# Trip of q, k, v and the attention output through memory: whole rows per block in place of strided pieces, with the features in another order

## The reference

```python
def _L1_attn_ref(x, Wqkv, Wproj, bproj):          # N_HEADS = 16, SCALE = 8.0
    qkv = jnp.einsum('bnm,fm->bnf', x, Wqkv)
    qkv = qkv.reshape(b, n, N_HEADS, -1)
    q, k, v = (qkv[..., :dh], qkv[..., dh:2 * dh], qkv[..., 2 * dh:])   # dh = 16
    scores = jnp.einsum('bnhd,bngd->bnhg', q, k) / SCALE
    attn = jax.nn.softmax(scores, axis=-1)
    out = jnp.einsum('bnhg,bngd->bnhd', attn, v)
    return jnp.einsum('bni,mi->bnm', out.reshape(b, n, -1), Wproj) + bproj

x = _layernorm(x + _L0_attn_ref(x, ...))
x = _layernorm(x + _L0_ffn_ref(x, ...))
x = _layernorm(x + _L1_attn_ref(x, ...))
x = _layernorm(x + _L1_ffn_ref(x, ...))
```

## Time and profile before

| | |
|---|---|
| runs | 1348.04, 1350.33, 1350.30 us; median 1350.3 |
| profiled execution | 1349.4 us, span 1347.6 us, granted clock 0.891 of full |
| busy in the span | PE 87%, DVE 70%, ACT 54%, POOL 42% |
| DMA | 90.64 MB in 94009 packets, most of them of 512 bytes |
| loads of 128 KB from `scratch_qkv` | 192 |
| stores of 512 KB to `scratch_qkv` | 48 |

### The profile page before, as it was taken

The page is one execution under the profiler, slowest core; times in us unless marked ns, Lnnn a source line. Parts: engine busy times, 40 slices in busy tenths (PEclk is TensorE's granted clock), DMA queues, the critical chain, the costliest instruction groups (busy, mean ns, idle before and its releaser), DMA issues.

```text
span 1347.6 us, 31178 instructions
## 1 busy us (share of the span) xinstructions
PE 1167.3 (87%) x12264; PEld 748.0 (56%) x12264; DVE 937.1 (70%) x2124; ACT 722.6 (54%) x1145; POOL 571.8 (42%) x882
## 2 busy tenths in 40 slices
PE   6688899998989999998999989898999988897464
PEld 4444466655665546655566556655566555654452
DVE  3544578677775868767775778668686777755866
ACT  3223375347753575547853477545754477544653
POOL 2235435335354355245354355354462352551124
PEclk8689898799979998799988999799987998799557
DMA  5000092203902075201902056021932029026430
GB/s 188 16 1 16 18 166 23 80 9 101 127 2 79 17 167 54 66 15 68 168 2 80 9 115 113 17 64 33 174 31 64 1 87 133 2 64 114 75 96 32
DMA packets 94009, 90.64 MB, mean 67 GB/s; under 512 B 7110, under 2 KB 83144, under 8 KB 93608
## 3 DMA queue, kind: packets, MB, share of 16 engines
q1 hardware_dynamic: 82008, 77.24, 29.3%
q0 software_dynamic: 2064, 6.69, 1.6%
q10 hardware_dynamic: 9792, 4.72, 1.4%
HBM read 46.68 MB, written 41.94 MB: 66 GB/s over the span
## 4 chain that ended last, share of the span: by engine, by line
PE 57%; DVE 18%; DMA 7%; issue 6%; ACT 5%; POOL 4%; ACTq 1%; SPq 1%; DVEq 0%; POOLq 0%
PE bank L1994 54%; DVE keys L1640 2%; DVE stats L1384 2%; DMA bt<-scratch_o 2%; DVE x L1525 2%; DVE gelu L1642 2%; POOL rs L655 2%; DMA scratch_o<-stage 2%; PE bank L2004 1%; ACT x L996 1%; DVE ct L1353 1%; DMA keys<-scratch_qkv 1%; ACTq L966 1%; ACT part L873 1%; DVE x L1708 1%
## 5 line engine op out<-in xcount | busy, mean ns | idle before, releaser
L1994 PE MATMUL bank<-we,at 128*128 128x512 f16 x1536 | 373.7, 403 | 1.9 <-DVE x L1525 1.9
L1994 PEld LDWEIGHTS bank<-we,at 128*128 128x128 f16 x1536 | 154.4, 102 | 194.6 <-issue 41.6
L670 POOL TENSOR_TENSOR part<-part 128x512 f32<-128x512 f32 x64 | 84.2, 1316 | 276.5 <-ACTq L1022 276.5
L873 ACT ACTIVATE part<-bank,wexp 128x256 f32<-128x256 f32 x256 | 104.3, 470 | 159.6 <-PE bank L1994 102.9
L1525 DVE SCALAR_TENSOR_TENSOR x<-bank,wexp,x 128x256 f32<-128x256 f32 x256 | 122.7, 479 | 53.0 <-PE bank L1994 46.5
L1994 PE MATMUL bank<-bt,wqkv 128*128 128x512 f16 x576 | 137.3, 380 | 20.8 <-DVE stage L1353 12.3
L996 ACT ACTIVATE x<-x,nm,rs 128x256 f32<-128x256 f32 x184 | 100.3, 593 | 69.3 <-POOL nm L658 68.1
L1353 DVE TENSOR_TENSOR stage<-bank,stage 128x512 f16<-128x512 f32 x110 | 74.4, 686 | 82.5 <-ACT stage L873 82.2
L651 POOL TENSOR_SCALAR nm<-mv 128x2 f32<-128x2 f32 x128 | 33.4, 261 | 207.1 <-DVE mv L1389 201.5
L1994 PE MATMUL bank<-keys,blockdiag 128*128 128x16 f16 x3072 | 97.5, 193 | 21.8 <-DVE blockdiag L1554 10.0
L1994 PEld LDWEIGHTS bank<-keys,blockdiag 128*128 128x128 f16 x3072 | 96.1, 103 | 26.4 <-issue 14.5
(11 more groups left out here) (212 smaller groups left out, 2275.4 us busy)
## 6 DMA issues: line engine op xcount, KB each, us to landing
scratch_qkv<-stage SPq DMA_DIRECT2D x39, 512.0 KB, 3.3
ct<-scratch_qkv SPq DMA_DIRECT2D x112, 128.0 KB, 6.5
x_in<-in_x_dram SPq DMA_DIRECT2D x32, 256.0 KB, 2.7
bt<-scratch_o SPq DMA_DIRECT2D x16, 512.0 KB, 4.1
keys<-scratch_qkv SPq DMA_DIRECT2D x61, 128.0 KB, 6.0
out_dram<-x POOLq DMA_DIRECT2D x24, 256.0 KB, 2.7
scratch_qkv<-part SPq DMA_DIRECT2D x8, 512.0 KB, 7.8
scratch_o<-stage SPq DMA_DIRECT2D x32, 128.0 KB, 3.5
```

Of the source, the lines that this page charges most:

```text
L670: pool.tensor_tensor(part[:, 0:2, :], part[:, 0:2, :], part[:, 2:4, :], ALU.add)\
L873: return act.activation(dst, src, ACT.Copy, scale=scale)
L1994: ins = pe.matmul(dst, lhs, rhs, start=(n == 0), stop=(n == len(terms) - 1))
```

## The change

The rows of the weights are put in another order on the host, so that within a block of 128 the features go by dimension, then head (q, k), or by head, then half of the dimensions (v). The block is stored as pieces of 512 bytes, 8 a partition, to a place r, p, n; read back as 128 rows of 4096 bytes, row 16 r + d then holds dimension d of group r for 8 heads. Each tensor comes back in two loads of 512 KB. The output makes the opposite way: two stores of whole rows, and two loads in pieces of 512 bytes. All of them are on SP; ACT's and POOL's issues go. The wait on POOL for v keeps its place and now counts two loads.

```diff
+            def half_of(home, ft):
+                return home[:, 2 * C * (ft % 2):2 * C * (ft % 2 + 1)]
...
+        def by_feature(memory):
+            return memory.rearrange("a m -> (a m)").rearrange("(r p n) -> p r n", r=T, p=P)
+        def qkv_block(ft):
+            return scratch_qkv[P * ft:P * (ft + 1)]
...   b_f and b_flast on SP
-                sp.dma_start(scratch_qkv[P * ft:P * (ft + 1)], slots[s]).then_inc(stored[s], 16)
+                sp.dma_start(by_feature(qkv_block(ft)), slots[s].rearrange("p (r n) -> p r n", r=T)).then_inc(stored[s], 16)
...
+            def load_block(b, ft, home, loaded):
+                sp.wait_ge(*f_stored(b, ft))
+                sp.sem_inc(waits_held, 1)
+                sp.dma_start(half_of(home, ft), qkv_block(ft)).then_inc(loaded, 16)
             def b_loadq(b):
+                if 0 < b < NB - 1:
+                    sp.wait_ge(ff_full, 4 * b)
                 for ft in (0, 1):
-                    (8 loads, or 4 for the last batch, on q_src[:, :, r, :])
+                    load_block(b, ft, q_home(b), q_loaded)
             def b_loads(b):
-                for ft in (0, 1, 3, 2):
+                for ft in (0, 1, 3):
                     b_flast(b, ft)
-                b_loadq(b)
+                load_block(b, 0, q_home(b), q_loaded)
+                b_flast(b, 2)
+                load_block(b, 1, q_home(b), q_loaded)
                 b_loadk(b)
-                (waits for k_loaded and k_rest)
+                sp.wait_ge(k_loaded, 32 * (b + 1))
                 sp.sem_inc(waits_held, 1)
                 for ft in (4, 5):
                     b_flast(b, ft)
                 b_loadv(b)
             def b_loadk(b):          # waits as before, then
-                for r in range(K_SP if b == NB - 1 else T):
-                    sp.dma_start(keys[DH * r:DH * (r + 1), :, :], ...)
+                for ft in ((3, 2) if b == NB - 1 else (2, 3)):
+                    load_block(b, ft, beats_keys, k_loaded)
             def b_loadv(b):
                 if b < NB - 1:
                     for hf in range(2):
                         sp.wait_ge(q_turned[hf], b + 1)
-                for r in range(T):
-                    sp.dma_start(home_rows(v_home(b), r), v_src[:, :, r, :]).then_inc(v_loaded, 16)
+                for ft in (4, 5):
+                    load_block(b, ft, v_home(b), v_loaded)
             def b_loado(b):          # waits as before, then
-                for r in range(T // 2):
-                    sp.dma_start(*o_store(r)).then_inc(o_stored, 16)
-                sp.wait_ge(o_stored, 128 * (b + 1))
                 for ht in range(KD):
-                    sp.dma_start(bt[:, ht, :, :]..., scratch_o[8 * ht:8 * ht + 8]...)
+                    sp.dma_start(scratch_o[P * ht:P * (ht + 1)], ohl[:, 8 * ht:8 * ht + 8, :, :]...)\
+                        .then_inc(o_stored[ht], 16)
+                for ht in range(KD):
+                    sp.wait_ge(o_stored[ht], 16 * (b + 1))
+                    sp.sem_inc(waits_held, 1)
+                    sp.dma_start(bt[:, ht, :, :]..., by_feature(scratch_o[P * ht:P * (ht + 1)])).then_inc(o_loaded, 16)
...   POOL, ACT and DVE
-                pool.wait_ge(v_loaded, 16 * T * (b + 1))
+                pool.wait_ge(v_loaded, 32 * (b + 1))
-            def b_loadk(b):          # POOL: 3 loads of k for the last batch
-            def b_storeo(b):         # ACT: 4 stores of the output
-            def b_loadq(b):          # ACT: 4 loads of q for the last batch
...   host
+    by_dim = _np.arange(D).reshape(2, 8, DH).transpose(0, 2, 1).reshape(-1)
+    by_head = _np.arange(D).reshape(HEADS, 2, 8).transpose(1, 0, 2).reshape(-1)
+    wqkv = wqkv[_np.concatenate([by_dim, D + by_dim, 2 * D + by_head])]
-        ("wproj_t", a["L1_attn_Wproj"].T),
+        ("wproj_t", a["L1_attn_Wproj"].T[by_dim]),
```

More of the change, by code:

```diff
@@ L222, in build_two_layer_postln @@
         o_hi = sem("o_hi")
-        o_stored = sem("o_stored")
+        o_stored = [sem(f"o_stored{ht}") for ht in range(KD)]
         o_loaded = sem("o_loaded")
@@ L437, in build_two_layer_postln @@
         out_d = out.rearrange("b (t p) d -> b p t d", p=P)
-        q_src, k_src, v_src = [scratch_qkv[D * n:D * (n + 1)].rearrange("(h d) (r n) -> h d r n", d=DH, r=T)
-                               for n in range(3)]
+        def by_feature(memory):
+            return memory.rearrange("a m -> (a m)").rearrange("(r p n) -> p r n", r=T, p=P)
+        def qkv_block(ft):
+            return scratch_qkv[P * ft:P * (ft + 1)]
         def places():
@@ L543, in b_loadk @@
             def b_loadk(b):
-                for ft in (2, 3):
-                    sp.wait_ge(*f_stored(b, ft))
-                    sp.sem_inc(waits_held, 1)
                 if b == NB - 1:
@@ L573, in b_loado @@
                 sp.sem_inc(waits_held, 1)
-                for r in range(T // 2):
-                    sp.dma_start(*o_store(r)).then_inc(o_stored, 16)
-                sp.wait_ge(o_stored, 128 * (b + 1))
-                sp.sem_inc(waits_held, 1)
                 for ht in range(KD):
-                    sp.dma_start(bt[:, ht, :, :].rearrange("p l n -> p (l n)"),
-                                 scratch_o[8 * ht:8 * ht + 8].rearrange("h d r n -> (h d) (r n)"))\
-                        .then_inc(o_loaded, 16)
+                    sp.dma_start(scratch_o[P * ht:P * (ht + 1)], ohl[:, 8 * ht:8 * ht + 8, :, :].rearrange("p h l n -> p (h l n)"))\
+                        .then_inc(o_stored[ht], 16)
+                for ht in range(KD):
+                    sp.wait_ge(o_stored[ht], 16 * (b + 1))
+                    sp.sem_inc(waits_held, 1)
+                    sp.dma_start(bt[:, ht, :, :].rearrange("p l n -> p (l n)").rearrange("p (r n) -> p r n", r=T),
+                                 by_feature(scratch_o[P * ht:P * (ht + 1)])).then_inc(o_loaded, 16)
             def b_store(b, p):
@@ L619, in _ @@
                 sp.wait_ge(*f_stored(NB - 1, ft))
-            sp.wait_ge(o_stored, 16 * T * NB)
+            for s in o_stored:
+                sp.wait_ge(s, 16 * NB)
             for s in out_stored:
@@ L706, in b_turnv @@
                                  turned(v_home(b), hf)).then_inc(v_turned[hf], 1)
-            def b_loadk(b):
[L709 to L716, removed]
             def b_s(b, q):
@@ L959, in b_o @@
                 copy(o_part(q, HI), o_psum(q)).then_inc(o_hi, 1)
-            def b_storeo(b):
[L962 to L966, removed]
             def b_spreadv(b, hf, rs):
@@ L1052, in b_spreadq @@
                     ins.then_inc(q_spread[1], 1)
-            def b_loadq(b):
-                for ft in (0, 1):
-                    act.wait_ge(*f_stored(b, ft))
-                for r in range(T // 2, T):
-                    act.dma_start(home_rows(q_home(b), r), q_src[:, :, r, :].rearrange("h d n -> d h n"))\
-                        .then_inc(q_loaded, 16)
             def b_gelu(b, p):
@@ L1129, in turn @@
                     to_at_hi(a, "TX0", 0, 0)
-                if c is not None:
-                    b_storeo(c)
                 if a is not None:
@@ L1563, in b_turnq @@
             def b_turnq(b, hf):
-                dve.wait_ge(q_loaded, 16 * T * (b + 1))
+                dve.wait_ge(q_loaded, 32 * (b + 1))
                 if b == NB - 1:
```

42 lines of the change are left out of this document (6 added, 36 removed).

## The result

The changed kernel takes 1352.8 us (median, 1349.6 to 1354.9) and the kernel before, run beside it, 1347.8. The ratio is 1.0039 with a 95% interval of 1.0026 to 1.0051: slower by 5.3 us, where +15.1 was forecast. The interval lies above the 0.2% that can be told from no change. The profiled execution after took 1354.8 us with a span of 1353.0; the one before 1349.4 and 1347.6. In what follows two of the twelve executions of experiment 3, at 2667 and 2669 us, are left out as slow ones.

A forecast was written before the change was run, and what follows sets the result against it. The prediction took PE as the bound, with over half of the chain of waits and DMA 7%. Costs of 28.7 less gains of 2.7, 2.0 and 8.9 gave +15.1, about 1365 us; range 1351 to 1380.

The forecast's parts named there:

- The mechanism: In seven turns v lands earlier, so GpSimd's copy starts amid VectorE's 8 spreads of q and holds them: 11 to 12 us.
- I let 3.7 stand: Scores start 3.7 us later in each of seven turns, 25.9 us, including 1.1 for GpSimd's next sum before the eighth spread.
- the two ends: Delay of the scores in a turn: 3.7 us with GpSimd's next sum holding the eighth spread, 2.6 without.
- The clock's term: More TensorE idle time ahead of the scores slows the expert matmuls: 0.4 us a turn, 2.8 us in all.
- rival D: Unseen slack behind the scores in the turn takes back half of the 25.9 us: 1352 us, chance 0.08.
- Last batch: Gains where nothing overlaps: q 4.0, v 2.0, output 2.4, ScalarE's and GpSimd's dropped issues 0.5; 8.9 us in all.
- v's 2.0: In the last batch v is there before it is asked for, so ScalarE's copy starts earlier: 2.0 us gained.
- the output's trip: In the turns it is 2.4 us shorter than 11.6, so TensorE's waits for it go: 2.7 us gained.
- the stores of the result: Result stores slowed beside q's stores get more of the engines beside small packets: 2.0 us gained, half of 2 x 2.0.
- B: GpSimd's copy of v does not hold VectorE back, or v misses the spreads; only gains stay: 1336.7 us, chance 0.14.
- C: 512-byte transfers run at 133 GB/s whatever their partitions, so output and q come later: 1386 us, chance 0.10.
- they alternate: GpSimd's instructions and VectorE's spreads do not share but take turns, each whole instruction holding the other; copy priced at 3.8 us.

The follow-up runs named there:

- experiment 3: Kernel before with the output's trip alone changed (two stores of whole rows, two loads in 512-byte pieces): 1340.3 us, ratio 0.9939.
- experiment 1: Changed kernel with one wait added: GpSimd's copies of v wait until the spreads of q are done: 1330.8 us, ratio 0.9876.
- experiment 11: Changed kernel with GpSimd's copy of v's first half moved behind its sum for the second tile, no wait added: 1330.5 us, ratio 0.9871.
- 9: Kernel of experiment 1 with a sum over 5440 columns added on VectorE ahead of the first spread of q: 1351.8 us, ratio 1.0026.
- experiments 5: Changed kernel with v's part undone (stores by whole rows, eight loads, old order): 1328.8 us, ratio 0.9862.
- experiment 8: Kernel of experiment 1 with the six q, k, v stores as whole rows, so it does not compute the reference: 1329.7 us, ratio 0.9866.
- 12: Changed kernel with v's part undone and GpSimd's copy of v's first half moved behind its sum for the second tile: 1329.8 us, ratio 0.9871.
- experiment 4: Kernel before with a sum over 2560 columns added on VectorE ahead of the second half of q's spreads: 1367.8 us, ratio 1.0126.
- experiment 2: Kernel before with v alone changed (stores in 512-byte pieces, two loads for eight, new feature order): 1359.2 us, ratio 1.0093.
- experiment 6: Kernel of experiment 1 with a sum over 3200 columns added on VectorE ahead of the first spread of q: 1333.9 us, ratio 0.9893.

## Why the prediction was right or wrong

**The mechanism was right.** In the like turn v is ready at the end of GpSimd's first sum (in two of the other turns the copy starts 0.3 or 0.4 us later); the copy starts 4.10 us behind the first spread (forecast 669.65 against 665.49, 4.16), holds one spread (4.26 us), and the 8 spreads take 10.88 (forecast 11 to 12). VectorE is 5.0 us late behind all twelve, as forecast. Experiments 1 and 11 take away the meeting and the harm goes; 9 puts the same delay back in another way, and it returns.

**The step that failed is "I let 3.7 stand".** Its 1.1 us for GpSimd's next sum, put ahead of the eighth spread, did not come true in the turns. I had the sum ready at 675.6 and the seventh spread ending at 675.8; the sum was ready as I said, but the spreads ran 0.2 us quicker than worked out, and the eighth began 0.05 us before the sum did. The sum then held the ninth. The scores moved by 2.57 us, which is the lower of the two ends I had named (2.6). That is 1.1 us less in each of six turns, 6.8 in all. In closing the sum did fall among the first eight: 4.9 us went at the scores, of which 4.0 reach the end. By the traces the harm is 17.1 + 4.0 = 21.1 us, by the medians of the changed kernel and experiment 1 it is 22.0, against 28.7: 6.7 of the 9.8 us by which the sum was off. The clock's term (0.4 a turn) was about right: the 2.1 us of busy time in six turns are 0.35 each, at a granted clock of 0.91 in the changed kernel's turns against 0.92 to 0.93.

A term that rests on which of two instructions is first by 0.2 us should have been split between both outcomes. By their middle, 3.15, the forecast would have been 11.3.

That 1352.8 lies within the stated range, 1351 to 1380, is owed to rival D alone, which set its low end; the forecast's own terms gave 1353 to 1376.

**The gains were 3.1 us too small.** By the ratio of experiment 1 they are 16.7 us, forecast 13.6.

- *Last batch:* forecast 8.9. In the traces, from the first spread of batch 6 to the end, it is 216.2 to 205.5 (experiment 1), 10.7 us. The pieces stand close to the forecast: from the first matmul on wqkv to the first scores 39.8 to 35.5, which is q's (4.3, forecast 4.0); over the scores 19.9 to 18.1 (1.8, v's 2.0); from there to the output's matmuls 33.0 to 30.5 (2.5, forecast 2.4). Of the rest 0.9 lies ahead of these pieces and 1.4 behind them, for which there was no term. v's gain does not need v's new loads: with v undone the scores take 18.1 too, and ScalarE turns v without idle time, as k is there sooner.
- *Turns:* 2.7 for the output's trip and 2.0 for the stores of the result, 4.7 in all. Six turns took 6.7 us less in experiment 1 and between 6.2 and 10.1 in experiments 5, 8, 11 and 12. Of this the output's part is as forecast (3.2 alone, experiment 3). The stores of the result are not where I looked: one still lies on experiment 1's chain with 5.29 us, against 4.75 in the earlier trace rows. Part of the rest is TensorE's own time: of experiment 1's 6.7 us, 3.5 are idle time of TensorE and 3.2 busy time (the three sums above). The turn of batch 3 in the windows view (stretch, length, busy time of each engine with instructions, granted clock, DMA share, GB/s), the kernel before and, below, experiment 11:

```profile
665.49:821.92 156.43, 143.60 (x1539) 92.22 (x1537) 114.91 (x263) 89.86 (x143) 72.19 (x109) 0.92 0.34 69
```

```profile
662.88:816.47 153.59, 141.96 (x1540) 91.99 (x1537) 114.66 (x264) 89.83 (x143) 72.11 (x109) 0.93 0.22 70
```

Of 2.84 us 1.64 are the same matmuls done quicker. Why the clock is granted a little earlier in some turns is not settled: turns of 153.4 and of 155.1 us stand side by side in one execution of experiment 1, with the same instructions, at granted clocks of 0.93 and 0.92, and no run varied the clock by itself.

**The sum.** 22.0 - 16.7 = +5.3. The forecast was 28.7 - 13.6 = +15.1.

**The rivals.** *B* (the copy does not hold the spreads) is out: they took 10.88 us. Its time without the meeting was 1336.7; the kernels without it run at 1329 to 1331. *C* (small pieces at 133 GB/s) is out: the output's trip of the last batch took 9.1 us from issue to landing (forecast 9.2, before 11.4), and the windows view of the loads' middle shows 284 GB/s on one queue.

```profile
1307.50:1310.50 3.00, 0.00 (x0) 0.00 (x0) 2.79 (x9) 3.00 (x8) 1.19 (x3) 0.50 0.99 284
```

*D* named the measured time, 1352, but not by its reason: there is no slack behind the scores that takes back half. The slack there is are the 1.04 us ahead of them, which the sum had counted, and some 3 us of VectorE's own behind them (experiment 4, three turns of one trace).

By the rule on 512 bytes that the prediction weighed (the Trainium skill, DMA: Bandwidth & Descriptors, section Specifications) such pieces cost a store nothing. The traces don't agree: a store is 0.5 to 0.6 us longer, near my 0.8, and the loads move 284 GB/s where whole rows moved 401. No effect on the time could be measured (experiment 8).

## What to carry to other kernels

A transfer that lands earlier releases its reader earlier, and the reader may belong among other work than it did: look at what each instruction behind a shortened load will lie beside, and on this chip at GpSimd beside VectorE's scalings first. Here an order of two GpSimd instructions was worth 22 us, more than all that the transfers gained. And when two traces differ less at the end of a turn than in its middle, try the harm by itself before calling the difference slack: here it was the gain of another part.

## What was not expected of the hardware

- An instruction that is held counts as busy: VectorE's busy time rose by 33.6 us with no change in its work, and the mean of the first group from 971 ns before to 1436. A group whose mean grows with the same shapes is a sign of a meeting.
- Which of the two is held can go by 0.05 us: GpSimd's next sum held the ninth and tenth spread in six turns and the seventh and eighth in the seventh turn. Nor is it always the spread: in experiment 2's closing the copy waited through three spreads and took 5.66 us. The forecast's "they alternate" holds for most meetings, not for all.
- The spreads were being held in the kernel before as well, as the prediction had read from the earlier trace rows; experiment 6 bears it out. With the sum over 3200 columns beside GpSimd's first three sums, the 8 spreads took 5.38 us in place of 7.36, and GpSimd's first sum 1.27 where 1.78 stands in the earlier trace rows.
- Stores of 512-byte pieces from 128 partitions land after 3.4 us where whole rows take 2.9 (medians of experiments 1 and 8), and loads of such pieces over 128 partitions move 284 GB/s, twice the 133 of 16 partitions.
